# Transformer decoder layer with cross attention, one core: the value matmuls of a cross unit in two runs of six groups in place of four of three, and a cross query stack of two batches in place of four

## Chip, cores and metric

One core of one Trainium2 chip. The metric is device time in microseconds (us). The kernel before was timed three times: 607.84, 609.78 and 613.45 us, median 609.78 us. One more execution of it was profiled, and all rows below are from that one.

## What is computed

Sixteen batches, 112 target rows and 375 source rows each, model width 256, 16 heads of 16 dimensions, hidden width 1024. Cut to what matters:

```python
x = layernorm(tgt, ln1); q, k, v = heads(x @ sa_wqkv)
sa = merge(softmax(q @ k.T * scale + causal + padding) @ v) @ sa_wproj + sa_bproj
result = tgt + sa
q2 = heads(layernorm(result, ln2) @ ed_wq)
k2, v2 = heads(layernorm(src, ln2) @ ed_wkv)
ed = merge(softmax(q2 @ k2.T * scale) @ v2) @ ed_wproj + ed_bproj
result = result + ed + relu(layernorm(tgt, ln3) @ ff_w1 + ff_b1) @ ff_w2 + ff_b2
```

## The kernel before

The sixteen batches are worked off in four groups of four (`BG = 4`). A group has eight attention **units**: self units 0 to 3 (one per batch, 112 keys, one chunk of keys) and cross units 4 to 7 (one per batch, 375 keys, three chunks of 125). Each unit is done in four **quarters** (u, g) of four heads. The units run in the order 2, 3, 4, 5, 0, 1, 6, 7, and this order of 32 quarters is a **turn** of the program, repeated about once per group; units 0 and 1 of a turn already belong to the next group.

A quarter has these steps. `score` multiplies keys and queries into one of two PSUM banks `scb` (L1092, L1097), and ScalarE takes the exponential into a slot of `prob` (L747); there are six slots. `pv` ("value matmuls", L1113) multiplies the values with the probabilities into the bank `pvb`. One pv step is a group of four matmuls, one per head, whose outputs lie at partitions 0, 32, 64 and 96. Each is fp32 and stands twice in the records, so a run of three groups has 24 records. `max` (L1078 for self, L1081 for cross) makes scores for the row maxima one unit ahead (`LEAD = 4` quarters) into one of three banks `mxb`, and VectorE reduces them (L882, L885): four reductions per quarter where the next unit is a cross one, which is so in units 3, 4, 1 and 6. GpSimd splits the maxima in three bf16 parts, `mT` (L1125) turns them on TensorE, and ScalarE copies them into rows of the query stack (L738), so that the score matmul subtracts the maximum by itself.

The rest of the layer is laid between these steps by a hand-written table, `other_work`, with a list for each quarter: `sT` transposes a source batch, `k2`, `v2` and `q2` are the cross projections (six matmuls each), `qk1` and `v1` those of self attention, `ff1` and `ff2` the feed-forward part, `o1`, `o2`, `o3` turn, normalise and project a unit's output. `period_steps` takes the steps of a quarter in rotation from three lists (its own, the maxima ahead, the other work), and every engine runs its part of the one resulting order.

All of these other steps, and `mT`, write to **two PSUM banks `misc` in strict rotation** (`MISC_BANKS = 2`): step n waits until the reader of step n-2 has released its bank. The reader is ScalarE or VectorE as listed in `MISC_READER`. For `k2` and `q2` the release comes late, because ScalarE first makes the first bf16 part (L732), and only then VectorE the remainder (L819), which releases the bank. For `sT` ScalarE makes the high part (L714) and then VectorE the low one (L812).

The parts of q, k, q2 and k2 are then moved by the DMA queue of SP into stacks (`q1st`, `k1st`, `q2st`, `k2st`), six transfers per step `stack_...`. `q2st` holds the queries of all four batches of a group, 16 heads by 448 columns. A self unit runs its four value groups together, behind its last quarter; a cross unit runs the three groups of a quarter one quarter later:

```python
        if u >= BG:
            run = [("pv", u, g, c) for c in range(chunks(u))]
        else:
            run = [("pv", u, h, 0) for h in range(4)] if g == 3 else []
```

## Time and profile before

| | |
|---|---|
| median of three timed runs | 609.78 us (607.84 to 613.45) |
| the profiled execution | 610.33 us |
| its span, first to last instruction | 608.3 us |
| mean granted TensorE clock | 0.979 of full speed |
| busy: TensorE matmul / weight load | 91% / 73% of the span |
| busy: VectorE / ScalarE / GpSimd | 66% / 54% / 18% |

In the rows, PE is TensorE's matmuls, PEld its weight loads, DVE is VectorE, ACT is ScalarE, POOL is GpSimd. A matmul's start is what is recorded, its end is modelled, so lengths of steps are read from start to next start. The third turn of the program, about 258 to 397 us from the span's start, is taken as the pattern: turns before and behind it repeat it.

### The profile page before, as it was taken

To read this page: it belongs to the slowest core of one execution; us is meant where nothing else is said; L and a number is where in the kernel's file an instruction comes from. 1 tells how busy PE (TensorE), PEld (TensorE's weight loads), DVE (VectorE), ACT (ScalarE), POOL (GpSimd) and SP (SyncE) were. 2 spreads that over 40 slices of the span, in tenths; PEclk is the share of its full clock that TensorE was granted. 3 is DMA by queue.
4 is the path that set the end of the run, shared out by engine and by line. 5 is a ranking of instruction groups with operands and counts; after the bars stand their busy time and mean duration, and the time that the engine had idled before them with its cause. 6 is when DMAs were issued, how large, how long until landed. Compare 5 with 4: busy or idle time off the path is not lost.

```text
span 608.3 us, 14162 instructions
## 1 busy us (share of the span) xinstructions
PE 551.4 (91%) x5564; PEld 445.1 (73%) x5564; DVE 402.9 (66%) x982; ACT 330.6 (54%) x615; POOL 110.1 (18%) x367
## 2 busy tenths in 40 slices
PE   3999877999999989899999999899999999999896
PEld 3887765768877877768877777768877777768674
DVE  7943767797477747696478747697568654685571
ACT  5626444266546746267546755357545665375183
POOL 2002312031023112031113112032113111130010
PEclk9869988999999999999999999999999999999998
DMA  8896077593650177392660168393570138104900
GB/s 234 172 133 121 20 118 112 84 116 70 121 123 1 46 107 114 69 127 57 121 135 6 46 84 122 66 123 62 115 119 13 32 81 135 35 3 89 125 2 16
DMA packets 74210, 52.84 MB, mean 87 GB/s; under 512 B 21984, under 2 KB 73376, under 8 KB 74144
## 3 DMA queue, kind: packets, MB, share of 16 engines
q1 hardware_dynamic: 74144, 51.94, 51.3%
q8 instruction: 44, 0.72, 0.6%
q14 instruction: 22, 0.18, 0.2%
HBM read 14.36 MB, written 1.84 MB: 27 GB/s over the span
## 4 chain that ended last, share of the span: by engine, by line
PE 72%; DVE 13%; ACT 8%; issue 3%; POOL 3%; DMA 1%; SPq 0%; DVEq 0%; POOLq 0%; ACTq 0%
PE misc L1142 9%; PE misc L978 9%; PE pvb L1113 9%; PE misc L980 7%; PE misc L979 7%; PE scb L1097 7%; PE mxb L1081 5%; PE misc L1149 5%; DVE negm L885 3%; DVE rem L819 2%; ACT prob L747 2%; PE misc L1120 2%; PE mxb L1078 2%; PE scb L1092 2%; PE misc L1034 2%
## 5 line engine op out<-in xcount | busy, mean ns | idle before, releaser
L747 ACT ACTIVATE prob<-scb 125x448 f32<-125x448 f32 (+1 forms) x256 | 134.8, 544 | 72.1 <-PE scb L1097 68.6
L885 DVE TENSOR_REDUCE negm<-mxb 112x1 f32<-112x375 f32 x256 | 129.4, 540 | 30.0 <-PE mxb L1081 28.8
L1081 PE MATMUL mxb<-k2st,q2st 96*112 96x375 bf16 x256 | 82.0, 338 | 5.7 <-DVE negm L885 5.4
L1097 PE MATMUL scb<-q2st,k2st 128*125 128x112 bf16 x768 | 74.7, 223 | 3.2 <-ACT prob L747 2.1
L1097 PEld LDWEIGHTS scb<-q2st,k2st 128*125 128x125 bf16 x768 | 65.7, 137 | 15.8 <-ACT prob L747 7.9
L819 DVE SCALAR_TENSOR_TENSOR rem<-misc,bcol,qkp 128x224 f32<-128x224 f32 (+2 forms) x64 | 37.5, 586 | 57.2 <-ACT qkp L732 57.0
L678 POOL CAST mparts<-negm 112x8 bf16<-112x8 f32 x64 | 12.5, 195 | 320.8 <-DVE negm L882 175.3
L1142 PE MATMUL misc<-wf,hT 128*112 128x256 f32 x256 | 60.6, 382 | 5.0 <-DVE rem L819 5.0
L1113 PE MATMUL pvb<-prob,v 125*17 125x112 f32 (+1 forms) x2048 | 65.0, 261 | 0.1
L732 ACT ACTIVATE qkp<-misc,bcol 128x224 bf16<-128x224 f32 (+2 forms) x64 | 35.8, 559 | 51.1 <-PE misc L980 51.1
L882 DVE TENSOR_REDUCE negm<-mxb 112x4 f32<-112x448 f32 x64 | 39.2, 616 | 29.1 <-PE mxb L1078 28.9
L1142 PEld LDWEIGHTS misc<-wf,hT 128*112 128x112 f32 x256 | 44.1, 177 | 16.2 <-DVE rem L819 7.4
L1113 PEld LDWEIGHTS pvb<-prob,v 125*17 125x17 f32 (+1 forms) x2048 | 44.2, 97 | 14.2 <-issue 9.8
L1081 PEld LDWEIGHTS mxb<-k2st,q2st 96*112 96x112 bf16 x256 | 32.7, 131 | 18.7 <-DVE negm L885 12.3
L738 ACT ACTIVATE q2st<-misc 24x896 bf16<-24x896 f32 x32 | 29.2, 911 | 23.1 <-PE misc L1125 22.5
L823 DVE TENSOR_TENSOR qkp<-rem,qkp 128x224 bf16<-128x224 f32 (+2 forms) x64 | 34.0, 530 | 2.2
L717 ACT ACTIVATE hT<-misc,bcol 128x448 f32<-128x448 f32 x32 | 20.3, 635 | 27.1 <-PE misc L980 27.1
L978 PE MATMUL misc<-wv_hi,xsT_hi 128*125 128x256 f32 x96 | 31.2, 325 | 1.4 <-DVE att L891 0.9
L738 ACT ACTIVATE q1st<-misc 24x896 bf16<-24x896 f32 x32 | 29.2, 911 | 5.2 <-PE misc L1125 4.6
L726 ACT ACTIVATE v<-misc 125x256 f32<-125x256 f32 x48 | 18.5, 385 | 19.3 <-PE misc L980 18.3
L978 PE MATMUL misc<-xsT_hi,wk_hi 128*128 128x376 f32 x64 | 24.5, 383 | 4.2 <-DVE xsT_lo L812 1.9
L1097 PEld LDWEIGHTS scb<-q1st,k1st 128*112 128x112 bf16 x256 | 23.9, 133 | 5.3 <-issue 0.3
(150 smaller groups left out, 1160.6 us busy)
## 6 DMA issues: line engine op xcount, KB each, us to landing
k2st<-qkp SPq DMA_DIRECT2D x192, 93.8 KB, 4.3
xs<-in_ctx SPq DMA_DIRECT2D x16, 375.0 KB
q1st<-qkp SPq DMA_DIRECT2D x48, 112.0 KB, 5.2
k1st<-qkp SPq DMA_DIRECT2D x48, 112.0 KB, 6.6
q2st<-qkp SPq DMA_DIRECT2D x96, 56.0 KB, 2.3
xn<-in_x SPq DMA_DIRECT2D x4, 448.0 KB, 8.0
tb<-in_x SPq DMA_DIRECT2D x8, 224.0 KB, 10.6
out<-ostage SPq DMA_DIRECT2D x16, 112.0 KB, 3.7
```

The costliest lines, as they stand in the source:

```text
L738: nc.scalar.activation(rows, bank[NROW:NROW + 3 * HH, 0:T].unsqueeze(1).broadcast_to([3 * HH, HH, T]), ACT.Copy).then_inc(s_read["act"], 1)
L747: nc.scalar.activation(prob[0:rows, n % PROB_SLOTS, :], scb[n % SCORE_BANKS][0:rows, 0:GH * T], ACT.Exp, scale=SCALE).then_inc(s_ex, 1)
L819: V.scalar_tensor_tensor(r[:, 0:n], bank[:, 0:n], bias, parts[:, 0, 0:n], ALU.add, ALU.subtract).then_inc(s_read["dve"], 1)
L882: V.tensor_reduce(negm[:, at, i * GH:(i + 1) * GH], mx[0:T, 0:GH * T].rearrange("p (h s) -> p h s", h=GH), axis=AX_X, op=ALU.max, negate=T ...
L885: V.tensor_reduce(negm[:, at, i:i + 1], mx[0:T, 0:S], axis=AX_X, op=ALU.max, negate=True).then_inc(s_mx, 1)
L978: M(dst, w_hi[:, k], x_hi[:, k], start=(k == 0), stop=False)
L979: M(dst, w_hi[:, k], x_lo[:, k], start=False, stop=False)
L980: mm = M(dst, w_lo[:, k], x_hi[:, k], start=False, stop=(k == KT - 1))
L1081: mm = M(mx[0:T, 0:S], q2st[0:NROW, i, b * T:(b + 1) * T], k2st[k2_place(q, b)][0:NROW, i, 0:S], start=True, stop=True)
L1097: mm = M(sc[0:rows, j * T:(j + 1) * T], ks, (q1st if u < BG else q2st)[:, h, b * T:(b + 1) * T], start=(u >= BG), stop=(u >= BG or j == GH ...
L1113: mm = M(pvb[32 * j:32 * j + VW, g * T:(g + 1) * T], vals, prob[0:rows, slot, j * T:(j + 1) * T], start=(c == 0), stop=(c == chunks(u) - 1))
L1142: mm = M(bank[0:T, 0:C], hT[:, f, b * T:(b + 1) * T], wf2[:, f, :], start=(f == 0), stop=(f == FT - 1))
```

## The change

A cross unit's value groups run in two runs of six in place of four runs of three: nothing after quarters 0 and 2, the groups of quarters 0 and 1 in quarter 2, those of quarters 2 and 3 in the next unit's quarter 0. The probabilities live longer, so `prob` has ten slots. `q2st` holds two batches (224 columns per head), so its clearing at the start covers half the elements. The queries of batches 0 and 1 can be stacked only when unit 7 has used those of 2 and 3, and these only when unit 5 is done, so the steps `stack_q2` move to quarters (2, 0) and (0, 0). To keep the four slots of `qkp` free, `k2` of batches 1 and 3 moves later in the table, and `v2` and `ff2` take its place.

```diff
-PROB_SLOTS = 6
+PROB_SLOTS = 10
@@ other_work
-        (2, 0): [("o3_late", 7), ("load_tb", 1), ("sT", 1, 0), ("sT", 1, 1)],
-        (2, 1): [("k2", 1, 0), ("stack_k2", 1, 0), ("ff1", 4), ("k2", 1, 1), ("stack_k2", 1, 1)],
+        (2, 0): [("stack_q2", 0, 0), ("o3_late", 7), ("stack_q2", 0, 1), ("load_tb", 1), ("sT", 1, 0), ("sT", 1, 1)],
+        (2, 1): [("ff1", 4), ("v2", 1, 0), ("ff1", 6)],
...
-        (0, 1): [("o1", 5), ("k2", 3, 0), ("stack_k2", 3, 0)],
-        (0, 2): [("ff2", 2), ("o2", 5), ("k2", 3, 1), ("stack_k2", 3, 1)],
+        (0, 1): [("o1", 5), ("ff2", 2)],
+        (0, 2): [("k2", 3, 0), ("stack_k2", 3, 0), ("o2", 5)],
@@ period_steps
-            run = [("pv", u, g, c) for c in range(chunks(u))]
+            run = [("pv", u, h, c) for h in (g - 1, g) for c in range(chunks(u))] if g % 2 else []
...
-    s += [("pv", u, 3, c) for c in range(chunks(u))] + [("ot", u), ("v1", 2), ("o1", u), ("v1", 3), ("o2", u)]
+    s += [("pv", u, h, c) for h in (2, 3) for c in range(chunks(u))] + [("ot", u), ("v1", 2), ("o1", u), ("v1", 3), ("o2", u)]
@@ buffers and waits
-        q2st = sb("q2st", [P, H, NT], BF16)
+        q2st = sb("q2st", [P, H, NH], BF16)
...
-                    stack(s, ("q2", q, h, s[3]), NH, q2st[:, :, h * NH:(h + 1) * NH], Q_PART,
-                          ("score", q - 1, BG + 2 * h + 1, 3, 2) if q else None)
+                    stack(s, ("q2", q, h, s[3]), NH, q2st, Q_PART,
+                          ("score", q, BG + 1, 3, 2) if h else ("score", q - 1, BG + 3, 3, 2) if q else None)
...
-                        mm = M(mx[0:T, 0:S], q2st[0:NROW, i, b * T:(b + 1) * T], k2st[k2_place(q, b)][0:NROW, i, 0:S], start=True, stop=True)
+                        mm = M(mx[0:T, 0:S], q2st[0:NROW, i, b % 2 * T:(b % 2 + 1) * T], k2st[k2_place(q, b)][0:NROW, i, 0:S], start=True, stop=True)
```

**TensorE in unit 4** (`scb` scores, `mxb` maxima, `misc<-ident,ot` is `o1`, `misc<-ident,att` is `o2`, `pvb` the value matmuls). Before:

```order
328 L1120 MATMUL misc1<-ident,ot 112x128 x4
329 L1113 MATMUL pvb<-prob,v20 17x112 x12
330 L1081 MATMUL mxb1<-k2st1,q2st 112x375
331 L1097 MATMUL scb0<-q2st,k2st0 125x112 x4
332 L1081 MATMUL mxb2<-k2st1,q2st 112x375
333 L1097 MATMUL scb1<-q2st,k2st0 125x112 x4
334 L1081 MATMUL mxb0<-k2st1,q2st 112x375
335 L1097 MATMUL scb0<-q2st,k2st0 125x112 x4
336 L1081 MATMUL mxb1<-k2st1,q2st 112x375
337 L1131 MATMUL misc0<-ident,att 128x112 x2
338 L1113 MATMUL pvb<-prob,v20 17x112 x12
```

The same place after the change:

```order
328 L1123 MATMUL misc1<-ident,ot 112x128 x4
329 L1100 MATMUL scb0<-q2st,k2st0 125x112 x4
330 L1084 MATMUL mxb1<-k2st1,q2st 112x375
331 L1100 MATMUL scb1<-q2st,k2st0 125x112 x4
332 L1084 MATMUL mxb2<-k2st1,q2st 112x375
333 L1084 MATMUL mxb0<-k2st1,q2st 112x375
334 L1100 MATMUL scb0<-q2st,k2st0 125x112 x4
335 L1084 MATMUL mxb1<-k2st1,q2st 112x375
336 L1134 MATMUL misc0<-ident,att 128x112 x2
337 L1116 MATMUL pvb<-prob,v20 17x112 x24
```

The first run of twelve instructions is gone from between `o1` and the scores, and the second has twenty-four.

**TensorE in unit 0** (`misc...<-xsT,wk2` is `k2`, `misc...<-ident,att` is `o2`, `misc...<-identb,mparts` is `mT`; the digit behind `misc` is the bank). Before:

```order
460 L1092 MATMUL scb0<-maskt,identb 112x448
461 L1097 MATMUL scb0<-q1st,k1st 112x112 x4
462 L1074 MATMUL mxb0<-identb,maskt 112x448
463 L1078 MATMUL mxb0<-k1st,q1st 112x112 x4
464 L1142 MATMUL misc0<-wf2,hT 112x256 x8
465 L1131 MATMUL misc1<-ident,att 128x112 x2
466 L1125 MATMUL misc0<-identb,mparts0 24x112
```

After the change (the `wf2,hT` row stands directly ahead of these):

```order
451 L1095 MATMUL scb0<-maskt,identb 112x448
452 L1100 MATMUL scb0<-q1st,k1st 112x112 x4
453 L1077 MATMUL mxb0<-identb,maskt 112x448
454 L1081 MATMUL mxb0<-k1st,q1st 112x112 x4
455 L981 MATMUL misc0<-xsT_hi,wk2_hi 128x376
456 L982 MATMUL misc0<-xsT_lo,wk2_hi 128x376
457 L983 MATMUL misc0<-xsT_hi,wk2_lo 128x376
458 L981 MATMUL misc0<-xsT_hi,wk2_hi 128x376
459 L982 MATMUL misc0<-xsT_lo,wk2_hi 128x376
460 L983 MATMUL misc0<-xsT_hi,wk2_lo 128x376
461 L1134 MATMUL misc1<-ident,att 128x112 x2
462 L1128 MATMUL misc0<-identb,mparts0 24x112
```

Before, the predecessor of `mT` in its bank was the end of `ff2`; now it is `k2`, with only `o2` between them.

## Rows read from the trace of the kernel before

**Rows 1.** The page: busy time by engine, and two groups of ScalarE (busy, mean ns).

```profile
PE 551.4 (91%) x5564; PEld 445.1 (73%) x5564; DVE 402.9 (66%) x982; ACT 330.6 (54%) x615; POOL 110.1 (18%) x367
...
L747 ACT ACTIVATE prob<-scb 125x448 f32<-125x448 f32 (+1 forms) x256 | 134.8, 544 | 72.1 <-PE scb L1097 68.6
...
L738 ACT ACTIVATE q2st<-misc 24x896 bf16<-24x896 f32 x32 | 29.2, 911 | 23.1 <-PE misc L1125 22.5
```

**Rows 2.** Timeline of TensorE, units 4 and 5: start us, length us, instruction.

```profile
260.12 0.96 PE L1113 MATMUL pvb<-prob,v 112*17 112x112 f32 x32
261.01 0.37 PE L1081 MATMUL mxb<-k2st,q2st 96*112 96x375 bf16 x1
...
262.51 0.33 PE L1081 MATMUL mxb<-k2st,q2st 96*112 96x375 bf16 x1
262.67 0.60 PE L1120 MATMUL misc<-ident,ot 128*112 128x128 f32 x4
263.20 0.77 PE L1113 MATMUL pvb<-prob,v 125*17 125x112 f32 x24
263.90 0.37 PE L1081 MATMUL mxb<-k2st,q2st 96*112 96x375 bf16 x1
264.11 0.39 PE L1097 MATMUL scb<-q2st,k2st 128*125 128x112 bf16 x4
...
278.90 0.61 PE L1120 MATMUL misc<-ident,ot 128*112 128x128 f32 x4
279.35 0.39 PE L1097 MATMUL scb<-q2st,k2st 128*125 128x112 bf16 x4
```

**Rows 3.** Timeline of the weight loads around the same run.

```profile
262.51 0.52 PEld L1120 LDWEIGHTS misc<-ident,ot 128*112 128x112 f32 x4
263.20 0.52 PEld L1113 LDWEIGHTS pvb<-prob,v 125*17 125x17 f32 x24 [0.17 <-issue]
263.90 0.13 PEld L1081 LDWEIGHTS mxb<-k2st,q2st 96*112 96x112 bf16 x1 [0.18 <-issue]
```

**Rows 4.** Busy time in units 4, 0 and 6: us, PE, PEld, DVE, ACT, POOL, clock.

```profile
258.78:272.90 14.12, 12.87 (x188) 9.46 (x186) 13.50 (x41) 8.63 (x17) 4.99 (x15) 1.00 1.15 127
...
292.16:306.78 14.62, 14.28 (x125) 11.85 (x124) 7.78 (x16) 7.47 (x14) 0.94 (x5) 1.00 0.60 113
...
319.16:335.57 16.41, 15.69 (x203) 12.16 (x201) 13.22 (x35) 10.37 (x20) 5.59 (x16) 1.00 0.02 7
```

**Rows 5.** Timelines of TensorE and VectorE in unit 2: a k2 bank and who waits.

```profile
362.90 0.41 PE L978 MATMUL misc<-xsT_hi,wk_hi 128*128 128x376 f32 x1 [0.45 <-DVE xsT_lo L812]
...
364.87 0.61 DVE L819 SCALAR_TENSOR_TENSOR rem<-misc,bcol,qkp 128x375 f32<-128x375 f32 x1 [1.59 <-ACT qkp L732]
...
365.54 0.44 PE L978 MATMUL misc<-xsT_hi,wk_hi 128*128 128x376 f32 x1 [0.16 <-DVE rem L819]
```

**Rows 6.** Timeline of TensorE in unit 2: two source transposes.

```profile
359.46 0.48 PE L1034 MATMUL misc<-ident,xs 125*128 125x125 f32 x3
...
361.11 0.54 PE L1034 MATMUL misc<-ident,xs 125*128 125x125 f32 x3 [0.74 <-DVE xsT_lo L812]
```

**Rows 7.** Timeline of TensorE in unit 0, from o2 to o3.

```profile
301.60 0.36 PE L1131 MATMUL misc<-ident,att 112*128 112x112 f32 x2
302.28 0.22 PE L1125 MATMUL misc<-identb,mparts 112*24 112x112 bf16 x1 [0.32 <-DVE tb L896]
302.43 0.44 PE L978 MATMUL misc<-xsT_hi,wk_hi 128*128 128x376 f32 x1
...
304.33 0.36 PE L978 MATMUL misc<-wv_hi,xsT_hi 128*125 128x256 f32 x1
...
305.12 1.10 PE L1149 MATMUL misc<-wpe,aT 128*112 128x256 f32 x4
```

**Rows 8.** Timeline of TensorE at the end: the last value run.

```profile
599.14 1.29 PE L1113 MATMUL pvb<-prob,v 125*17 125x112 f32 x24
```

**Rows 9.** Timeline of VectorE in the opening: the query stack is cleared.

```profile
15.71 3.04 DVE L939 MEMSET q2st<- 32x3584 f32 x1 [0.82 <-issue]
```

More of the change, by code:

```diff
@@ L162, in of_next @@
             return t[1] in (0, 1) or (t[1] == UNITS[0] and kind in ("max", "max_parts", "mT") and at[t] > len(s) // 2)
-        if kind in ("q2", "stack_q2"):
+        if kind == "stack_q2":
+            return False
+        if kind == "q2":
             return t[1] == 0
@@ L736, in act_part @@
                     b = u % BG
-                    rows = (q1st if u < BG else q2st)[NROW:NROW + 3 * HH, half * HH:(half + 1) * HH, b * T:(b + 1) * T]
+                    c = slice(b * T, (b + 1) * T) if u < BG else slice(b % 2 * T, (b % 2 + 1) * T)
+                    rows = (q1st if u < BG else q2st)[NROW:NROW + 3 * HH, half * HH:(half + 1) * HH, c]
                     nc.scalar.activation(rows, bank[NROW:NROW + 3 * HH, 0:T].unsqueeze(1).broadcast_to([3 * HH, HH, T]), ACT.Copy).then_inc(s_read["act"], 1)
@@ L1096, in pe_part @@
                         ks = k1st[:, h, b * T:(b + 1) * T] if u < BG else k2st[k2_place(q, b)][:, h, c * SC:(c + 1) * SC]
-                        mm = M(sc[0:rows, j * T:(j + 1) * T], ks, (q1st if u < BG else q2st)[:, h, b * T:(b + 1) * T], start=(u >= BG), stop=(u >= BG or j == GH - 1))
+                        mm = M(sc[0:rows, j * T:(j + 1) * T], ks, (q1st[:, h, b * T:(b + 1) * T] if u < BG else q2st[:, h, b % 2 * T:(b % 2 + 1) * T]), start=(u >= BG), stop=(u >= BG or j == GH - 1))
                     mm.then_inc(s_sc, 1)
```

16 rows, old and new, of the table fill are left out of this document.

## Prediction

> **What bounds the kernel now.** Read the page first. TensorE is busy for 91% of the span, VectorE for 66% and ScalarE for 54% [rows 1]. So TensorE's order of work is the bound, in most places. Then read busy time by stretch, one stretch per unit, because a mean hides where this is not so. In unit 4 VectorE is busy for 13.50 of 14.12 us, TensorE for 12.87: there VectorE is the bound, because it must reduce 16 maxima for unit 5 as well as normalise. In unit 0 TensorE has 14.28 of 14.62 us. Unit 6 lies between: TensorE 15.69, VectorE 13.22 of 16.41 us [rows 4]. Last read TensorE's timeline for what costs it time without being work. Two things show: a gap each time it enters or leaves a value run, and waits for one of the two misc banks.
>
> **What a value run costs beyond its matmuls.** A run of 24 records takes 0.70 us to the next start (263.20 to 263.90), one of 32 records 0.89 us (260.12 to 261.01) [rows 2]. So one group of 8 records costs 0.19 us, and 0.70 - 3 x 0.19 = 0.13 us is paid once at the run's end. At its beginning, o1 takes 0.53 us when a value run follows (262.67 to 263.20) and 0.45 when a score follows (278.90 to 279.35): 0.08 us. The maximum behind a run takes 0.21 us (263.90 to 264.11), elsewhere 0.16 (262.51 to 262.67): 0.05 us [rows 2]. Together 0.25 us a run (rounded down; 0.26 by these rows). The weight loads say the same: they pause 0.17 us on entering and 0.18 us on leaving [rows 3]. There are 16 cross units, each with two runs fewer: 32 x 0.25 = 8.0 us, 2.0 us in each of four turns. That is the gain if TensorE bounds everywhere and nothing new waits.
>
> A rule of the Trainium skill speaks against it. What the rows show: the loads for o1 run from 262.51 on, while the maximum of 262.51 is still in flight, and only at the two edges of the value run does loading stop [rows 2, 3]. The page "TensorE: Matmul & The Clock Gate", section "The mechanism" of its part on packing small matmuls, says that a weight load overlaps matmuls in flight only when its row group differs. The value matmuls use all rows, so by this rule no load here would overlap anything, an edge of a run would cost nothing extra, and the gain would be nil. The trace disagrees with it for ordinary steps, so I give that case little.
>
> **What is lost in unit 4.** TensorE gives up one run's three groups there (3 x 0.19 = 0.57 us, done later in unit 5) and the edges of two runs (0.50), 1.07 us. VectorE's reductions stay, and it has only 14.12 - 13.50 = 0.62 us of idle [rows 4]. So unit 4 can shorten by 0.6 at most; I take 0.5. The 0.57 comes back further on, where TensorE is the bound (unit 5 hands three groups on in its turn, and unit 0 has three more than before). Loss against the 2.0: +0.57 per turn.
>
> **New waits for the misc banks.** The distance that matters is from a k2's start to the earliest start of the step that uses its bank next. Where that step was waiting, it was 365.54 - 362.90 = 2.64 us, and the remainder on VectorE (364.87 + 0.61 = 365.48) released it [rows 5]. For a source transpose it is 361.11 - 359.46 = 1.65 us [rows 6]. The k2 itself fills about 1.1 us of this (302.43 to 304.33 less some 0.8 for the score and the maximum between, by their four records of about 0.2 [rows 7]), so the work between it and the next user of its bank must cover 1.5 us.
> - Unit 0, mT behind k2: between them stands only o2 (about 0.4 us, its own row's length being 0.36). mT starts 2.64 us after k2, where TensorE arrives after 1.1 + 0.4: a wait of 1.1 us. Before, it waited for ff2's bank, 301.60 to 302.28 in place of 0.4, so 0.27 [rows 7]. Net +0.85.
> - Unit 0, o3 behind the second k2: before, a score, a maximum and v2 stood between (302.43 to 305.12 is 2.69 us, just enough). Now only v2 (304.33 to 305.12, 0.79): arrival after 1.91, wait 0.7 [rows 7]. Net +0.7.
> - Unit 0, mT behind two source transposes which now follow one another: due at 1.65, arrival at 0.8 us; a third of this was waited for before as well. Net +0.6.
> - Unit 5: v2 behind k2 with mT, score and maximum between (0.75 us): wait 0.8. k2 behind q2, whose value run between them is gone: 0.35. Against that the order of o2, k2 and mT is turned there, which frees about 0.6. Net +0.55.
> - Unit 2: k2 moves away from the transposes it waits for now (0.45 us ahead of 362.90, 0.74 ahead of 361.11 [rows 5, 6]), but mT comes to stand two steps behind k2 (0.75). Adding up both orders row by row gives -0.5.
>
> Sum +2.2 per turn: unit 0 +2.15, unit 5 +0.55, unit 2 -0.5.
>
> **Units 6 and 7.** Here maxima and scores wait now and then behind a value run; with longer stretches without one VectorE and ScalarE get their input sooner. VectorE leaves 3.2 us of unit 6 free [rows 4], so the shortening is allowed. Bounds: nothing, or 1.5 us. I take -0.7.
>
> **The sum.** A full turn: -2.0 + 0.57 + 2.2 - 0.7 = +0.07; three of them +0.2. The last turn has no scores of units 0 and 1: edges -2.0, unit 4 +0.5, units 0 and 5 +1.7 (k2 now directly behind k2 in its bank, the third bullet unchanged), unit 2 -0.5. At the very end the last value run takes 1.29 in place of 0.70 us because it waits for exponentials [rows 8]; with the groups of quarter 2 ahead of it that wait is covered: -0.6, and -0.3 more in units 6 and 7. Together -1.2. In the opening the clearing of the stack (3.04 us [rows 9]) halves; the remainder that follows waits for it, but would soon wait for ScalarE: between 0 and -1.5, I take -0.7. Total +0.2 - 1.2 - 0.7 = -1.7 us.
>
> Moved transfers cost nothing as I read it: the query stacks for units 6 and 7 are filled in unit 0, those for 4 and 5 in unit 2, each a whole unit (14.62 us for unit 0 [rows 4]) before their first maximum. What SP's queue holds behind them, k2's stacks and loads for later units, has as long. Without this cover the first maximum of a unit would wait for the landing, and TensorE with it.
>
> The profiled execution took 610.33 us, the median is 609.78, 0.55 less. 610.33 - 1.7 - 0.55 = 608.1, so **608 us**. Its own range, from the bounds above (units 6 and 7: 0.7 x 3 either way, opening 0.7, bank waits a third wrong, 2 x 3), is 604 to 612. A measurement here tells about 1%, 6 us, from no change.
>
> **Rivals.**
> 1. *The gain arrives whole.* The bank waits fall where TensorE would have waited anyway, or the readers run ahead because fewer maxima are queued; unit 4 is not held by VectorE, since its idle time only counts what the trace calls idle. For it: 8.0 us is firmly measured per edge. Against it: 13.50 of 14.12 us [rows 4], and the 2.64 us distance is set by two engines' latencies, not their load [rows 5]. Then -8.0 - 0.7 and about -0.5 for unit 2: 601 us. Chance 0.26.
> 2. *Bunched scores: slower.* In the four quarters of units 4 and 6 that lose their value run, three scores follow one another with maxima alone between. ScalarE needs for them three exponentials of 0.544 us and a copy of 0.911 us for mT [rows 1], 2.5 us, while TensorE's own work sinks to about 1.8 us (o1 0.45, four maxima of 0.16 and three scores, taken as 0.2 [rows 2]), and there are two score banks only. Up to 0.7 us is lost in each, and the following quarter with six groups is TensorE's 0.6 us longer, so it isn't made up. In unit 4 this hides under VectorE. If unit 6 cannot make it up, nor units 5 and 7 in their quarters, that is 4 x 4 x 0.4 = 6.4 us: 614.5 us. It decides once a quarter without value matmuls takes over 2.5 us in unit 6. Chance 0.22.
> 3. *The change doesn't save what it says:* the edge is no cost of the run but of whatever stands there (the rule above). Then all 8.0 are missing: 616 us. Chance 0.05.
>
> The forecast has 0.47. Faster by over 1%: rival 1 and a little of the forecast's own width, 0.28. Within 1%: 0.47. Slower by over 1%: rivals 2 and 3, less their near ends, 0.25. The range 600 to 615 takes in rival 1 and most of rival 2.
>
> **What would show it.** In the profile after: value runs of 48 records from start to next start in 6 x 0.19 + 0.13 = 1.27 us (right) or 1.40 (edges cost nothing). Idle of TensorE for VectorE's remainder L819, now about 1 us ahead of mT and 0.7 ahead of o3 in unit 0. Unit 4 at 13.5 to 13.7 us with VectorE over 95% busy; unit 0 at about 17.4 us (14.62 + 2.15 + 0.57 and rounding); unit 6 near 14.8, of which 0.57 is only moved. Unit 4 below 13 us, or unit 0 below 16, makes the prediction wrong towards rival 1; unit 6 above 16 towards rival 2; a TensorE wait for a query stack would be a cause I did not price.

## The result, and the profile after

The changed kernel takes **652.13 us** (median of four timed runs, 650.83 to 653.19) against 608.82 for the kernel before beside it (607.84 to 613.45): a ratio of 1.068, with a 95% interval of 1.0637 to 1.0726. The forecast was 608 us with a range of 600 to 615. It is slower by 7%, outside everything that was priced.

The page of the kernel after: busy time, granted clock, the chain that ended last, and the groups that answer to [rows 1].

```profile
PE 550.7 (85%) x5564; PEld 452.6 (70%) x5564; DVE 401.6 (62%) x982; ACT 327.9 (50%) x615; POOL 110.2 (17%) x367
...
PE 50%; DVE 15%; SPq 10%; ACT 10%; DMA 8%; issue 4%; POOL 3%; DVEq 0%; ACTq 0%; POOLq 0%
SPq L569 9%; DMA q2st<-qkp 8%; PE misc L1145 7%; PE misc L981 7%; PE pvb L1116 6%; PE misc L983 5%; PE misc L982 5%; PE scb L1100 4%; PE mxb L1084 4%; DVE rem L822 3%; DVE negm L888 3%; PE misc L1152 3%; ACT qkp L734 3%; ACT prob L750 2%; DVE stats L798 2%
...
L750 ACT ACTIVATE prob<-scb 125x448 f32<-125x448 f32 (+1 forms) x256 | 135.3, 546 | 67.8 <-PE scb L1100 64.9
...
L1128 PE MATMUL misc<-identb,mparts 112*24 112x112 bf16 x64 | 14.2, 222 | 46.0 <-DVE rem L822 36.1
```

Read the busy times first: they are what they were (551.4, 402.9 and 330.6 us [rows 1]), so no engine got more work. Then the chain: SP's queue and the landing of the query stacks hold 17% of it. Last, where TensorE stands: `mT` waits 36.1 us for the remainder of a split. The remainder waits in its turn. The waits after, by line waited for: total us, times, longest us.

```profile
DVE rem L822 <- ACT qkp L734: 81.3, 47, 8.4
...
ACT qkp L734 <- DMA q2st<-qkp: 41.6, 8, 8.1
PEld misc L1128 <- DVE rem L822: 38.1, 11, 8.1
PE misc L1128 <- DVE rem L822: 36.1, 11, 7.9
```

Eight times ScalarE stood before the first bf16 part of a split (L732 before, L734 after), 41.6 us in all, until a query stack had landed: 7 to 8 us in unit 2 of each turn, 1 to 2 us in unit 0 of three turns, and 7.2 us in unit 5 of the last turn. That is as much as the loss (650.4 - 608.3 = 42.1 us of span); how far it is the loss, the experiments must tell. The place is seen in unit 2. TensorE's timeline after:

```profile
385.30 0.42 PE L981 MATMUL misc<-xsT_hi,wk_hi 128*128 128x376 f32 x1
...
387.00 0.28 PE L983 MATMUL misc<-wv_hi,xsT_lo 128*125 128x256 f32 x1
395.19 0.27 PE L1128 MATMUL misc<-identb,mparts 112*24 112x112 bf16 x1 [7.91 <-DVE rem L822]
395.38 0.74 PE L981 MATMUL misc<-xT_hi,wf_hi 128*128 128x448 f32 x1
```

ScalarE's timeline beside it, with the split of that `k2`:

```profile
385.25 0.54 ACT L750 ACTIVATE prob<-scb 112x448 f32<-112x448 f32 x1
393.85 0.58 ACT L734 ACTIVATE qkp<-misc,bcol 128x375 bf16<-128x375 f32 x1 [8.06 <-DMA q2st<-qkp]
```

SP's queue, issues only, and the transfer in the chain of that stretch:

```profile
373.09 8.76 SPq L569 DMA_DIRECT2D k2st<-qkp  x12
381.89 0.49 SPq L584 DMA_DIRECT2D xs<-in_ctx  x1
382.43 3.82 SPq L569 DMA_DIRECT2D q2st<-qkp  x6
386.29 0.59 SPq L599 DMA_DIRECT2D out<-ostage  x1
```

```profile
385.64 8.12 DMA q2st<-qkp
393.80 0.05 issue
393.85 0.59 ACT qkp L734
394.48 0.04 issue
394.52 0.62 DVE rem L822
```

`qkp` has four slots, used in the order of the splits: q2 0 0, q2 0 1, k2 0 0, k2 0 1, and then k2 1 0, which takes the slot of q2 0 0. That slot is free only when the stack made from it has landed. Before, SP issued this stack in unit 7, far ahead of that k2 (362.90 [rows 5]). SP's queue before:

```profile
340.38 8.33 SPq L567 DMA_DIRECT2D q2st<-qkp  x12
...
354.35 7.86 SPq L567 DMA_DIRECT2D k2st<-qkp  x12
```

After, it issues them from 382.43 on, 5.6 us into unit 2, at 0.64 us a transfer (3.82 us for six), behind the twelve transfers of k2's stacks (373.09 to 381.85) and one load of a source batch. The place in the query stack was free from about 372.4 on, when unit 7's last score was done. The last of the six starts at 385.64 and lands 8.12 us later, while k2 has been on TensorE since 385.30. Each of these two delays is large: 10 us in the queue, 8 us on the way. Of the same six transfers the first four land after 4.1 to 4.6 us, the last two after 7.9 and 8.1. Behind k2's split ScalarE holds the value copy and VectorE the release of the misc bank for which `mT` waits, so everything stops. Unit 0 has the same with k2 3 0.

There is a second price. Busy time by stretch, unit 2 after (us, PE, PEld, DVE, ACT, POOL, clock, share of DMA, GB/s):

```profile
376.85:401.29 24.44, 16.06 (x97) 13.37 (x96) 8.27 (x22) 8.46 (x16) 2.85 (x10) 0.80 0.71 118
```

The granted clock is 0.80 in this stretch, and 0.50 from 395 to 401 us. Behind the 7.91 us in which TensorE stood, a matmul of 448 columns takes 0.57 in place of 0.36 us, and the next one starts 0.37 in place of 0.20 us later: that is the lower of the two levels, 1.2 GHz. The same 97 rows are busy for 13.28 us in the first experiment below, at clock 1.00; so the wait adds 2.8 us of slower work to its own length. Unit 2 is 10.0 us longer than in that run (24.44 and 14.44): 7.91 - 0.68 us of waiting at this `mT`, and the slower work.

Steps against the kernel before, per unit of one turn (start to next start, us; the turn that begins at 218.87 before):

| unit | before | after | stack alone (e4) | fifth slot (e1) | runs alone (e3) |
|---|---|---|---|---|---|
| 2 | 15.24 | +7.73 | +7.52 | -0.82 | +0.02 |
| 3 | 24.67 | +0.06 | +0.44 | +1.56 | +0.04 |
| 4 | 14.12 | -0.50 | -0.02 | -0.51 | -0.51 |
| 5 | 19.27 | +0.42 | 0.00 | +0.37 | +1.25 |
| 0 | 14.62 | +5.43 | +4.24 | +2.82 | +0.57 |
| 1 | 12.38 | 0.00 | 0.00 | +0.02 | 0.00 |
| 6 | 16.42 | -1.11 | -0.01 | -1.11 | -1.11 |
| 7 | 22.19 | +0.49 | -0.03 | +0.49 | +0.58 |
| sum | | +12.5 | +12.1 | +2.8 | +0.8 |

In all four turns unit 2 loses 6.80, 7.73, 9.21 and 6.81 us.

### The profile page after: what moved, and what is told of

The parts are those of the page before. It is cut to its first block, busy times and chain, and to the rows that moved or that the text cites. A ratio compares the mean times of both kernels' runs of the same rounds, so it can differ in the third digit from the quotient of the medians.

```text
span 650.4 us, 14090 instructions
## 1 busy us (share of the span) xinstructions
PE 550.7 (85%) x5564; PEld 452.6 (70%) x5564; DVE 401.6 (62%) x982; ACT 327.9 (50%) x615; POOL 110.2 (17%) x367
## 3 DMA queue, kind: packets, MB, share of 16 engines
HBM read 14.36 MB, written 1.84 MB: 25 GB/s over the span
## 4 chain that ended last, share of the span: by engine, by line
PE 50%; DVE 15%; SPq 10%; ACT 10%; DMA 8%; issue 4%; POOL 3%; DVEq 0%; ACTq 0%; POOLq 0%
SPq L569 9%; DMA q2st<-qkp 8%; PE misc L1145 7%; PE misc L981 7%; PE pvb L1116 6%; PE misc L983 5%; PE misc L982 5%; PE scb L1100 4%; PE mxb L1084 4%; DVE rem L822 3%; DVE negm L888 3%; PE misc L1152 3%; ACT qkp L734 3%; ACT prob L750 2%; DVE stats L798 2%
## 5 line engine op out<-in xcount | busy, mean ns | idle before, releaser
L1100 PE MATMUL scb<-q2st,k2st 128*125 128x112 bf16 x768 | 76.3, 223 | 7.5 <-ACT prob L750 7.5
L1084 PE MATMUL mxb<-k2st,q2st 96*112 96x375 bf16 x256 | 78.9, 335 | 3.4 <-DVE negm L888 3.0
L734 ACT ACTIVATE qkp<-misc,bcol 128x224 bf16<-128x224 f32 (+2 forms) x64 | 35.7, 558 | 87.4 <-PE misc L983 45.8
L680 POOL CAST mparts<-negm 112x8 bf16<-112x8 f32 x64 | 12.5, 195 | 352.9 <-DVE negm L885 178.7
L1116 PE MATMUL pvb<-prob,v 125*17 125x112 f32 (+1 forms) x2048 | 59.5, 262 | 0.0
L1128 PE MATMUL misc<-identb,mparts 112*24 112x112 bf16 x64 | 14.2, 222 | 46.0 <-DVE rem L822 36.1
L1116 PEld LDWEIGHTS pvb<-prob,v 125*17 125x17 f32 (+1 forms) x2048 | 46.8, 98 | 8.9 <-issue 6.8
L1128 PEld LDWEIGHTS misc<-identb,mparts 112*24 112x24 bf16 x64 | 5.7, 89 | 59.7 <-DVE rem L822 38.1
L757 ACT ACTIVATE ot<-pvb 128x448 f32<-128x448 f32 x32 | 17.4, 545 | 27.9 <-PE pvb L1116 27.9
```

The source lines that it names most:

```text
L734: nc.scalar.activation(parts_of(s)[:, 0, 0:n], misc_bank(s)[:, 0:n], ACT.Identity, bias=bcol[:, col:col + 1]).then_inc(s_p1, 1)
L1084: mm = M(mx[0:T, 0:S], q2st[0:NROW, i, b % 2 * T:(b % 2 + 1) * T], k2st[k2_place(q, b)][0:NROW, i, 0:S], start=True, stop=True)
L1100: mm = M(sc[0:rows, j * T:(j + 1) * T], ks, (q1st[:, h, b * T:(b + 1) * T] if u < BG else q2st[:, h, b % 2 * T:(b % 2 + 1) * T]), start=(u ...
L1116: mm = M(pvb[32 * j:32 * j + VW, g * T:(g + 1) * T], vals, prob[0:rows, slot, j * T:(j + 1) * T], start=(c == 0), stop=(c == chunks(u) - 1))
```

## The experiments

All ratios are to the kernel before on the same chip, with the 95% interval.

**The late stack: e1, e2, e4.** A fifth slot for `qkp`, so that k2 1 0 no longer needs the slot of q2 0 0:

```diff
-PROB_SLOTS = 10
-SPLIT_TILES = 4
+PROB_SLOTS = 9
+SPLIT_TILES = 5
```

> The changed kernel with five qkp slots in place of four (SPLIT_TILES 5, and PROB_SLOTS 9 to make room). Theory A (the first part of a k2 waits on ScalarE until the query stack that was made from the same qkp slot has landed, and the queries' transfers now stand late in SP's queue): with five slots the first k2 behind the queries takes a slot that has long been free, and the second k2 waits for it about 14 us later, when it has landed. ScalarE's wait for q2st (41.6 us after the change) falls below 6 us, unit 2 from 24.4 to 15-17 us, unit 0 from 20.0 to 17-18, the clock there is full again, the whole 612 to 620 us. Rival B (the new order of k2, v2 and ff1 over the two misc banks costs it): nothing of that depends on the qkp slots, so 645 us or more. Rival C (transfers of the smaller stack are slow and disturb everything): 640 us or more, since the same transfers run.

620.45 us, 1.0164 [1.013, 1.0199]: 31.7 of the 43.3 us are gone with one slot. That is at the edge of what theory A expected (612 to 620) and far from both rivals. Waits of e1:

```profile
ACT qkp L734 <- DMA q2st<-qkp: 7.8, 3, 2.8
...
PE misc L1128 <- DVE rem L822: 7.9, 11, 1.2
```

ScalarE waits 7.8 in place of 41.6 us. Most of what is left stands in units 0 and 3. Unit 0 is the misc banks, below. In unit 3 the first maximum now comes before its query stack has landed, because unit 2 is shorter: TensorE's timeline of e1, first steps of unit 3.

```profile
377.69 0.37 PE L1100 MATMUL scb<-q1st,k1st 128*112 128x112 bf16 x4
379.51 0.34 PE L1084 MATMUL mxb<-k2st,q2st 96*112 96x375 bf16 x1 [1.45 <-issue]
```

The row names no releaser. What that maximum reads is the first of the two query stacks, and SP's queue of e1 issues it here:

```profile
368.79 3.82 SPq L569 DMA_DIRECT2D q2st<-qkp  x6
```

By the landing times in the trace its last transfer starts at 372.00 and lands at 379.42, 7.4 us later; the maximum starts at 379.51. The same landing releases ScalarE's one wait of this turn (2.61 us, until 379.50).

Second, the twelve transfers ahead of it in SP's queue, taken away by stacking k2 of batch 0 as soon as it is split:

```diff
-        (7, 1): [("o1", 6), ("q2", 0, 1), ("k2", 0, 0), ("ff1", 3)],
-        (7, 2): [("k2", 0, 1), ("o2", 6), ("stats_s", 1), ("v2", 0, 0)],
-        (7, 3): [("v2", 0, 1), ("o3", 6), [("stack_k2", 0, 0), ("stack_k2", 0, 1)], ("norm_s", 1), ("v2", 0, 2), ("load_src", 2)],
+        (7, 1): [("o1", 6), ("q2", 0, 1), ("k2", 0, 0), ("stack_k2", 0, 0), ("ff1", 3)],
+        (7, 2): [("k2", 0, 1), ("stack_k2", 0, 1), ("o2", 6), ("stats_s", 1), ("v2", 0, 0)],
+        (7, 3): [("v2", 0, 1), ("o3", 6), ("norm_s", 1), ("v2", 0, 2), ("load_src", 2)],
```

> The changed kernel with the k2 stacks of batch 0 put directly behind their k2 in unit 7, in place of unit 7's end. Same slots, same work, same banks on TensorE; only SP's queue differs: its 12 transfers of 0.6 us no longer stand ahead of the queries' in unit 2. Theory A: queries' transfers start with unit 2 and land before the k2 needs the slot; unit 2 falls to 15-18 us in all four turns, about -25 to -32 us in all: 620 to 627 us. The wait in unit 0 (about 1.5 to 3 us a turn) stays. Rival B and C: within 3 us of 652.

631.95 us, 1.0352 [1.0328, 1.0377]. Unit 2 loses 5.93 us in the first turn and between -0.52 and +0.18 in the others; `ACT qkp L734 <- DMA q2st<-qkp: 15.9, 3, 7.5` are its waits. The expectation, 620 to 627, was too low: one wait in unit 2 and the one in the last turn stay. So the queue's order is about half of the cause (20.2 of 43.3 us): the same four slots suffice in most turns if SP reaches the stack sooner, but with no margin.

What stays in e2 is the length of the landing. The source load still stands directly ahead of the stack there, and the last two of its six transfers still take 4.9 to 7.2 us. Where it goes out with no source load directly ahead, its six transfers land in 2.2 to 2.9 us (before, from 340.38 on; after, from 599.52 on). That the load makes the landing long fits these times, but no run moves the load, so it is not shown. In the last turn of the kernel after the stack lands in 2.3 us, and ScalarE waits 7.2 us all the same (7.5 in e2): with no units 0 and 1 behind unit 5, k2 follows closely, while unit 5's last score (594.2) and then twelve transfers of k2's stacks (until 598.8) hold the query stack back.

Third, the change without its runs: four runs of three as before, the small stack and the new table as after.

```diff
-            run = [("pv", u, h, c) for h in (g - 1, g) for c in range(chunks(u))] if g % 2 else []
+            run = [("pv", u, g, c) for c in range(chunks(u))]
...
```

> The changed kernel with the old value runs of three groups: two-batch query stack, new table, ten slots. Theory A: it has the whole loss and lacks the gain: 652 + 3 to 8 = 655 to 660 us, with the same waits of ScalarE for q2st (about 40 us). If the longer value runs were what shifts the queries' stacks late: 615 to 640 us.

652.91 us, 1.0704 [1.0664, 1.0744]: as slow as the whole change and a little faster than expected (655 to 660), with `ACT qkp L734 <- DMA q2st<-qkp: 39.4, 6, 7.9`. The small stack and its table are the loss. This kernel also measures the misc banks apart from longer runs: unit 0 loses 2.25 us, forecast 2.15, in the two turns in which no stack is late.

**The runs of six alone: e3.** The kernel before, with the stack of four batches and its table, seven slots for `prob`; six small constants lie in `aT` during the opening to make room.

```diff
-PROB_SLOTS = 6
+PROB_SLOTS = 7
-            run = [("pv", u, g, c) for c in range(chunks(u))]
+            run = [("pv", u, h, c) for h in (g - 1, g) for c in range(chunks(u))] if g % 2 else []
...
```

> The kernel before with the value runs of six groups and nothing else of the change: the four-batch query stack and the old table stay. There is room for seven probability slots only, and for them five small tensors of the opening lie in a tile that is first used later. If the price of an edge of a run (0.25 us) counts wherever TensorE bounds, and unit 4 is held by VectorE: -3 to -6 us against before, 603 to 606. If all 32 runs count: 601. If bunched scores cost more than the edges: 609 to 615. A control for the slots: with seven of them a score may wait for its slot; then ScalarE's exponentials wait for value matmuls in the trace.

613.04 us, 1.006 [1.0038, 1.0081]: slower by half a per cent, where the edges alone say -8 us. Of the three ranges expected it is the one for scores that meet (609 to 615). Its stretches, units 4, 5, 0, 6 and 7 (columns as above), show where they arrive and where not.

```profile
258.62:272.23 13.61, 12.08 (x164) 9.06 (x162) 12.99 (x40) 8.65 (x17) 4.97 (x15) 1.00 1.18 126
272.23:292.74 20.51, 18.75 (x239) 16.22 (x239) 13.54 (x36) 13.21 (x28) 4.14 (x15) 1.00 0.50 67
292.74:307.92 15.18, 14.78 (x148) 12.41 (x147) 7.77 (x16) 7.45 (x14) 0.93 (x5) 1.00 0.82 115
...
320.30:335.61 15.31, 14.74 (x181) 11.70 (x179) 12.46 (x34) 9.93 (x20) 5.55 (x16) 1.00 0.01 3
335.61:358.37 22.76, 21.45 (x298) 18.60 (x297) 14.66 (x38) 14.75 (x32) 3.34 (x14) 1.00 0.20 50
```

Unit 6 gives up three groups (0.57) and two runs (0.50) and is 16.41 - 15.31 = 1.10 us shorter [rows 4]: there the edge has its full price. Unit 0 is longer by three groups and nothing else (15.18 - 14.62 = 0.56). Unit 4 gives 0.51 of 1.07, as forecast for a unit that VectorE holds. Unit 5 should give 0.50 and loses 1.25; unit 7, which runs its own last six groups at its end (+0.57 - 0.50), should lose 0.07 and loses 0.58. The last two are the error here. In unit 5 `v1` waits for the output of `o3` on VectorE, in unit 7 the first source transpose waits for the normalised source. TensorE's timeline of e3:

```profile
290.26 0.28 PE L979 MATMUL misc<-wv_hi,xT_lo 128*112 128x256 f32 x1
291.23 0.38 PE L977 MATMUL misc<-wv_hi,xsT_hi 128*125 128x256 f32 x1 [0.69 <-DVE ostage L905]
```

```profile
337.11 0.51 PE L1033 MATMUL misc<-ident,xs 125*128 125x125 f32 x3 [0.72 <-DVE xs L806]
```

and VectorE's before the first of these:

```profile
289.26 1.05 DVE L806 TENSOR_SCALAR xs<-xs,mv,rstd 125x256 f32<-125x256 f32 x3
290.23 0.62 DVE L881 TENSOR_REDUCE negm<-mxb 112x4 f32<-112x448 f32 x1
290.76 0.41 DVE L905 TENSOR_TENSOR ostage<-misc,tb 112x256 f32<-112x256 f32 x1
```

`ostage`, for which a misc bank waits, stands in VectorE's order behind a normalisation that nobody needs until unit 0.

**Is it the table? e5.** e1 and e2 together, and quarters 1 to 3 of units 0 and 2 from the table before:

```diff
-        (2, 1): [("ff1", 4), ("v2", 1, 0), ("ff1", 6)],
+        (2, 1): [("k2", 1, 0), ("stack_k2", 1, 0), ("ff1", 4), ("k2", 1, 1), ("stack_k2", 1, 1)],
...
-        (0, 1): [("o1", 5), ("ff2", 2)],
-        (0, 2): [("k2", 3, 0), ("stack_k2", 3, 0), ("o2", 5)],
+        (0, 1): [("o1", 5), ("k2", 3, 0), ("stack_k2", 3, 0)],
+        (0, 2): [("ff2", 2), ("o2", 5), ("k2", 3, 1), ("stack_k2", 3, 1)],
...
```

> The kernel after with three things undone or taken away: five slots for qkp (nine for prob), the stacks of k2 of batch 0 directly behind their k2, and the lists of other work for quarters 1 to 3 of units 0 and 2 as in the kernel before (the query stacks stay where the change put them, in quarter 0). Theory A: of the 42 us, about 39 are the wait of ScalarE for a landed query stack before it may fill the same slot of qkp; what then is left of units 0's loss is the misc banks' waits, which belong to the table. By it this kernel is close to the runs of six alone (e3: 613.0), unit 0 costs +0.6 us a turn against before in place of +2.8, unit 2 between -0.8 and +0.3, ScalarE's waits at L734 for q2st add up to under 8 us: 611 to 615 us. Theory B: the smaller query stack costs time whatever the table, since six stacks more stand in SP's queue ahead of loads and k2 stacks in quarter 0: then unit 0 and unit 2 stay 2 us or more above before in each turn, 620 to 630 us.

618.04 us, 1.011 [1.0072, 1.0149], above the range of theory A (611 to 615) and below that of theory B (620 to 630). Unit 0 costs +1.17 in place of +2.82 us a turn, so most of its loss is the table's. But in the first turn unit 2 again loses 6.71 us (`ACT qkp L734 <- DMA q2st<-qkp: 10.5, 2, 9.0`): k2 comes earlier here, and five slots no longer cover a landing that takes 8.8 us. (In the first turn the query stack again stands behind k2's twelve transfers and a source load.)

**Is it the misc banks? e6, e7.** e1 and the kernel before, each with a third misc bank taken from the maxima:

```diff
-MISC_BANKS, MAX_BANKS, SCORE_BANKS = 2, 3, 2
+MISC_BANKS, MAX_BANKS, SCORE_BANKS = 3, 2, 2
```

> The kernel of e1 (after, with five slots for qkp) and three misc banks in place of two, paid for with one of the three banks of maxima. Theory A (unit 0 loses 2.2 us a turn because mT and o3 stand right behind a k2 in the two-bank rotation): with a third bank unit 0 falls by 1.8 to 2.4 us a turn against e1; the maxima with two banks cost up to 0.5 us in each of units 3, 4, 1 and 6, where a quarter makes four of them. 614 to 622 us against 620.5 for e1. Theory B (unit 0's loss is the arrival of work from ScalarE and VectorE, not the bank): unit 0 stays within 0.5 us of e1 and the sum is 620 us or more.

> The kernel before with three misc banks and two banks of maxima: the control of e6. If the loss in unit 0 is one the changed order makes, unit 0 gains here at most its present waits for a bank (0.3 us ahead of mT, and up to 0.7 us behind the source transposes), far less than in e6; units with four maxima a quarter lose up to 0.5 us each. 605 to 614 us. If a third bank gives 2 us in unit 0 here as well, e6 says nothing about the change.

e6 takes 615.32 us, 1.006 [1.0024, 1.0095]; e7 607.78 us, 0.9947 [0.9919, 0.9976]. Unit 0 falls from 17.44 to 14.78 us in e6, by 2.66, and from 14.62 to 14.08 in e7, by 0.54. TensorE's timeline of unit 0 in e1:

```profile
297.41 0.86 PE L1037 MATMUL misc<-ident,xs 125*128 125x125 f32 x6
299.11 0.22 PE L1128 MATMUL misc<-identb,mparts 112*24 112x112 bf16 x1 [0.83 <-DVE xsT_lo L815]
305.87 0.36 PE L1134 MATMUL misc<-ident,att 112*128 112x112 f32 x2
307.41 0.22 PE L1128 MATMUL misc<-identb,mparts 112*24 112x112 bf16 x1 [1.18 <-DVE rem L822]
311.03 1.12 PE L1152 MATMUL misc<-wpe,aT 128*112 128x256 f32 x4 [0.67 <-DVE rem L822]
```

and the same steps in e6:

```profile
290.73 0.86 PE L1037 MATMUL misc<-ident,xs 125*128 125x125 f32 x6
291.51 0.22 PE L1128 MATMUL misc<-identb,mparts 112*24 112x112 bf16 x1
298.31 0.36 PE L1134 MATMUL misc<-ident,att 112*128 112x112 f32 x2
298.60 0.22 PE L1128 MATMUL misc<-identb,mparts 112*24 112x112 bf16 x1
301.70 1.02 PE L1152 MATMUL misc<-wpe,aT 128*112 128x256 f32 x4
```

All three waits named in the prediction stand in e1 and are gone with a third bank. The maxima pay with two banks: against the kernel before, +0.57 in unit 4 and +0.60 in unit 1 of most turns of both, +1.3 in unit 6 of e7. Against e1 itself, e6 pays 1.1 us in unit 4 and 1.9 in unit 6. e6 keeps the late stack (`ACT qkp L734 <- DMA q2st<-qkp: 15.6, 5, 4.3`), and the runs behind its ratio spread from 609.8 to 617.8 us.

**Versions of the kernel before: e8, e9.** e8 moves one step:

```diff
-        (2, 1): [("k2", 1, 0), ("stack_k2", 1, 0), ("ff1", 4), ("k2", 1, 1), ("stack_k2", 1, 1)],
+        (2, 1): [("ff1", 4), ("k2", 1, 0), ("stack_k2", 1, 0), ("k2", 1, 1), ("stack_k2", 1, 1)],
```

> The kernel before, with one step of the table moved: in quarter (2, 1) ff1 4 stands ahead of k2 1 0. In the trace of before k2 waits there 0.45 us for the second source transpose's low part on VectorE, and the next bank user 0.16 us; the one saving that I foresaw in unit 2 of the change was this. Theory A: the wait is covered by ff1, -0.3 to -0.9 us in each of four turns, 606 to 609 us. Theory B: k2's chain through ScalarE and VectorE comes later by the length of ff1, and the next maximum or mT waits for it: within 0.3 us a turn of before or above it, 609 to 612 us.

> The kernel before with e7 and e8 together: three misc banks, two banks of maxima, and ff1 4 ahead of k2 1 0. If both took the same wait of k2 for a bank in unit 2, unit 2 stays where e7 has it (14.05 us) and the time is that of e7, 606 to 608 us; if they are separate, unit 2 falls by another 0.5 us a turn, 604 to 606 us.

e8: 607.76 us, 0.9947 [0.9917, 0.9977], -0.48 us in unit 2 in three of four turns. e9, which is e7 and e8 together: **603.27 us, 0.9884 [0.985, 0.9917]**, better than either kernel of this case. Unit 2 falls by 2.4 us in three of four turns, more than the 1.2 of e7 and the 0.5 of e8 together: with ff1 first and a third bank k2 finds both its source and its bank. The expectation, 604 to 606, was too high.

**Where the edges' saving goes: e10 to e18.** e10 is e9 with runs of six, e3's edit. e11 is e3 and e12 the kernel before, both with

```diff
-MISC_BANKS, MAX_BANKS, SCORE_BANKS = 2, 3, 2
+MISC_BANKS, MAX_BANKS, SCORE_BANKS = 2, 2, 3
```

> Runs of six with the stack of four batches (e3), and three misc banks, two banks of maxima, ff1 4 ahead of k2 1 0. Against e9 it differs by the longer runs alone. Theory A: what the runs lose in units 5 and 7 (1.25 and 0.58 us a turn in e3) are waits for a misc bank; with a third bank the edges' saving of 2.0 us a turn shows at last in units 5, 0 and 7: 600 to 604 us. Theory B: they are latencies and queues of ScalarE and VectorE that the spread-out value runs used to cover; then it is as far above e9 as e3 is above before, or at most level with it: 605 to 611 us.

> The kernel of e3 (runs of six, stack of four batches) with three score banks and two banks of maxima. Theory A: the edges' 8 us in e3 are eaten by scores which follow one another and wait for an exponential to free one of two banks (in its trace these waits of TensorE grew from 2.1 to 8.2 us, 9 to 23 of them). With a third bank they go, and against its control (e12) this kernel is 4 to 8 us faster. Theory B: a score that goes ahead only meets the next engine in the chain (VectorE's remainders, the misc banks); then this kernel is within 3 us of e12 or slower. Both contain the cost of the missing bank for maxima: 608 to 618 us.

> The kernel before with three score banks and two banks of maxima, the control of e11. Its scores wait only 2.1 us in all, so the third bank gains at most that; the missing bank for maxima costs, as in e7, about +0.6 in units 4 and 1 and +1.3 in unit 6 a turn, near 10 us over four turns: 613 to 620 us by either theory.

e10: 610.51 us, 1.0004 [0.998, 1.0027], 7.2 us above e9. e11: 631.05 us, 1.0364 [1.0338, 1.039]; e12: 623.11 us, 1.0226 [1.02, 1.0252]. A third misc bank doesn't bring the saving to light, nor does a third score bank, though it removes the waits of scores for exponentials: 8.2 us in e3, 1.2 in e11. I had expected e11 to beat e12 by 4 to 8 us; it is 8 us slower, and that theory falls. Both also lie above their ranges (608 to 618 and 613 to 620): the missing bank for maxima costs more than was taken. In e11 the wait for `ostage` at the end of unit 5 stands as it did (0.7 us in each of three turns).

So VectorE's order was moved, in e3 (e13), before (e14), e9 (e15) and e10 (e16):

```diff
-        (5, 2): [("q2", 1, 1), ("stack_q2", 1, 1), ("v2", 2, 0), ("o2", 4), ("k2", 2, 1), ("stack_k2", 2, 1), ("norm_s", 3)],
-        (5, 3): [("v2", 2, 1), ("o3", 4), ("v1", 0), ("v2", 2, 2), ("load_src", 0), ("v1", 1)],
-        (6, 3): [("norm2", 1), ("ff1", 0), ("norm_s", 0), ("xq", 1)],
+        (5, 2): [("q2", 1, 1), ("stack_q2", 1, 1), ("v2", 2, 0), ("o2", 4), ("k2", 2, 1), ("stack_k2", 2, 1)],
+        (5, 3): [("v2", 2, 1), ("o3", 4), ("norm_s", 3), ("v1", 0), ("v2", 2, 2), ("load_src", 0), ("v1", 1)],
+        (6, 3): [("norm_s", 0), ("norm2", 1), ("ff1", 0), ("xq", 1)],
```

> The kernel of e3 (runs of six, stack of four batches) with two normalisations of a source batch moved in the table: norm_s 3 behind o3 4 in quarter (5, 3), norm_s 0 ahead of norm2 1 in quarter (6, 3). Theory A: TensorE's saved edges in units 5 and 7 are eaten because VectorE's queue is late there: in e3 v1 waits 0.69 us for ostage, which stands behind xs (1.05 us), and the first sT of unit 7 waits 0.72 us for xs. With both moved, units 5 and 7 together lose at least 1.2 us a turn less: 607 to 610 us, and the gain against e14 is 0.5 to 1.5 us a turn larger than that of e3 against before. Theory B: it is the misc banks and ScalarE there, not VectorE's order: within 2 us of e3.

> The kernel before with the same two normalisations moved, the control of e13. In before v1 waits for nothing there, and the first max of unit 7 takes 0.65 us in place of e3's 1.28, so little is to be had: within 2 us of before by either theory, 607 to 611 us.

> The kernel of e9 with the two normalisations moved. If VectorE's order isn't what holds e9: 602 to 605 us. Unit 6 of e9 waits for maxima, which xs placed earlier can lengthen by up to 0.5 us a turn.

> The kernel of e10 (runs of six on e9) with the two normalisations moved. Theory A (VectorE's order eats the edges): at or below e15, 600 to 605 us. Theory B: 608 us or more, as e10.

| | us | ratio |
|---|---|---|
| e13 | 613.67 | 1.0054 [1.0025, 1.0083] |
| e14 | 607.64 | 0.9957 [0.9934, 0.9979] |
| e15 | 603.19 | 0.9883 [0.9841, 0.9926] |
| e16 | 611.23 | 1.002 [0.9999, 1.0041] |

In e13 the two waits are gone: unit 5 is at +0.33 and unit 7 at -0.32, together 1.8 us better than e3, as theory A wants. Yet the time stays (expected were 607 to 610), mostly because unit 6 went from 15.30 to 16.52 us; unit 2 loses another 0.7 and 1.1 us in two of the turns, which stays open. TensorE's timeline of e13 there:

```profile
334.51 0.44 PE L1096 MATMUL scb<-q2st,k2st 128*125 128x112 bf16 x4 [1.16 <-ACT prob L746]
```

The rotation of the three lists now set ff1 behind the scores instead of between them, and ScalarE had three exponentials in a row. This was my edit's doing; one list entry in place of two puts ff1 back (e17; e18 is its control, on the kernel before):

```diff
-        (6, 3): [("norm_s", 0), ("norm2", 1), ("ff1", 0), ("xq", 1)],
+        (6, 3): [[("norm_s", 0), ("norm2", 1)], ("ff1", 0), ("xq", 1)],
```

> The kernel of e13 with norm_s 0 and norm2 1 as one entry of the list of quarter (6, 3), so that ff1 0 stands between two scores again; in e13 three scores followed one another there and the third waited 1.16 us for an exponential. Theory A: unit 6 is back at 15.3 us (16.52 in e13) while units 5 and 7 keep what they gained, so -1.2 us in each of three turns and about as much less in unit 7's start: 608 to 610.5 us. Theory B: xs placed this early costs VectorE's maxima of unit 7 the same 1.2 us in another place: 612 us or more.

> The kernel before with the same moves as e17, its control. With runs of three, a value run parts the scores in any case, so it stays near e14: 606.5 to 609 us. If e17 comes out below this kernel by 2 us or more, the edges' saving is real once the waits are gone; level or above means that they are still eaten, by at least the 8 us less the difference.

e17: 608.87 us, 0.997 [0.9951, 0.9988], and e18: 609.61 us, 0.9974 [0.9955, 0.9993]. Unit 6 is back at 15.40. With the two waits of e3 and the meeting of scores of e13 out of the way, runs of six are level with runs of three, 4.2 us better than e3. In the units that hold the moved groups e17 gains 0.55 us a turn on e18 (second turn): unit 6 -0.99, unit 4 -0.49, unit 7 -0.06, against +0.58 in unit 0 and +0.41 in unit 5. With everything else, above all 1.1 us lost once in unit 2 and 0.9 gained once in unit 3, the four turns stand at -1.3, +0.5, -0.1 and +0.3 us. Of the 2.0 us a turn 1.45 are still not seen: 0.6 in unit 4 (VectorE) and 0.9 in unit 5. There two scores take 0.55 and 0.59 us to the next start in e3, and as long in e17, in place of 0.28 and 0.27. Behind the first stands a maximum that waits for a reduction on VectorE; only the second is a wait for an exponential (0.20 us). That removing them would give the 0.9 back was not shown.

## Why the prediction was wrong

**The step that failed: "Moved transfers cost nothing as I read it."** It weighed only who reads the moved stack: the first maximum, a whole unit later. It left out who needs what the stack reads *from*, and how late SP's queue reaches the stack. The query stack's transfers hold a slot of `qkp`; four splits later ScalarE must write that slot. The diff itself said that the table moved "to keep the four slots of qkp free", and I took the new distance for enough without counting it: k2 1 0 starts at 385.30, the stack's last transfer begins at 385.64 and lands at 393.8. The price is 6.8 to 9.2 us in unit 2 each turn, 30.6 us in all, 2.7 us in unit 5 of the last turn (+4.53 there against +1.84 in e1), and 2.6 in one unit 0 (5.43 against 2.82). The cover that the same step did count on, a whole unit before the first maximum, is too short as well: in e1 the stack goes out 5.7 us into unit 2 and lands 16.4 us into it, the unit takes 14.4 us, and the first maximum waits 1.45 us. The prediction did name the sign to look for, a wait for a query stack that was not priced.

The other terms can be read in e1, where that wait is small. They too come out worse than their sum: e1's span is 9.0 us above before, where -1.7 was forecast. Unit 3 is 5.3 of that over four turns, units 6 and 7 some 1.1 a turn, and the last turn 1.6.

- **Edges.** A run of 48 records was forecast at 1.27 us; TensorE's timeline of the kernel after has one from 307.33 to the next start at 308.61, 1.28 us. Unit 6 of e3 is 1.10 us shorter, 1.07 by the prediction's row arithmetic. The edge's 0.25 us is right there, and an edge that costs nothing would have given 0.57. The Trainium skill's rule that a weight load overlaps only where the row group differs ("TensorE: Matmul & The Clock Gate", "The mechanism") is the one from which the prediction drew that case; the same section also lets a load run ahead into a background weight buffer, which the prediction left out, and which would fit the loads for o1 that run under the maximum of 262.51 [rows 2, 3]. Another page of the Trainium skill bears on it: "TensorEngine Tiling (Array Packing)", section "Key Properties", says that changing the tiling mode drains TensorE. The pauses of 0.17 and 0.18 us in the weight loads [rows 3] fit that; no run here tells a drain from another cause.
- **Misc banks in unit 0.** Forecast 1.1 us ahead of `mT`, 0.7 ahead of `o3` and a wait behind the transposes; measured 1.18, 0.67 and 0.83. Unit 0 was to be "about 17.4"; it is 17.44 in e1. e6 confirms the cause.
- **Unit 4.** 13.61 us, forecast 13.5 to 13.7, with VectorE busy for 12.99 in e3: rightly the bound.
- **Unit 5.** Forecast +0.05 (edges -0.50, banks +0.55), measured +0.37 in e1 in the second turn. That is two errors that nearly meet: the runs alone cost +1.25 there (e3), not -0.50, and the rest of the change takes 0.9 back in place of adding 0.55.
- **Unit 2 without the late stack:** -0.8 against -0.5.
- **Units 6 and 7.** Forecast -1.7 together with their edges (-1.0 and -0.7), measured -0.6. The extra -0.7 was the wrong sign: readers don't get ahead; what value runs covered comes open in unit 7.
- **Unit 3** was not spoken of, and loses 1.6 to 2.1 us in three turns of e1, where its first maximum waits for the first query stack.
- **The last turn** was put at -1.2; e1 has +0.4 there (unit 2 -0.81, unit 4 -0.77, unit 5 +1.84, unit 6 +0.38, unit 7 -0.29).
- **The opening** gained 1.85 us in the kernel after and 0.8 in e1, forecast 0.7; the clearing took 1.55 for 3.04 us [rows 9]. But the opening also came out 1.6 us shorter in e14, which clears the old stack, so the gain is not shown to be the clearing's.

Rival 2 had the mechanism that later bit in e13, scores which meet because no value run stands between them, but with a size of 0.4 us in four quarters; in unit 6 of e3, where it was placed, nothing of it shows. None of the rivals had the cause.

## What to carry to other kernels

When a transfer is moved, count at both its ends: who reads the target, and who next writes the source. A ring of n slots turns a transfer's delay into a wait of the n-th producer behind it, which here sat on ScalarE in front of the whole chain. Count also what stands ahead of the transfer in its queue: here 10 us passed between the moment when the stack was free to go and the moment when SP reached it.

Fillers that cost the bounding engine time may be what lets the others keep up: the value runs' edges cost 8 us by the row, and taking them away alone made the kernel 3 us slower, and only level with its control once normalisations and scores had been placed anew. The best kernels found here keep runs of three: e9 (603.27 us) changes banks and one step only, and e15 (603.19 us) is level with it.

## What the runs showed of the hardware that was not expected

- A transfer of the query stack takes 2.3 us from issue to landing in the median before and 3.6 after, but 8.12 us in the case shown, where SP's queue had sent the twelve transfers of k2's stacks and a source load directly ahead. The median on the page says nothing about the one that is waited for.
- SP's queue needs 0.60 us and 0.04 us between for each of these transfers; twelve hold it for 7.6 us at least, and for 8.76 us ahead of the stack shown.
- A wait of 7.91 us costs more than its length: the granted clock of the stretch falls to 0.80, matmuls of 448 columns start 0.37 to 0.38 us apart in place of 0.20, and those of 376 columns 0.31 in place of 0.17. After the shorter wait of 2.27 us in unit 0 the same is seen, and the stretch has 0.91. In e1, where that unit has waits of 0.67 to 1.18 us, its stretch has 1.00.
